# A two-layer graph network on one core: fewer semaphore signals per tile, and a node's own row as one product and one sum over types

## What is computed

```
h = max(layernorm(x), 0)
for l in range(3):                                   # W_rel (3, 8, 256, 256)
    xr  = einsum('nd,rde->rne', h, W_rel[l])
    msg = xr[edge_type, src]
    agg = segment_sum(msg, dst)
    h   = relu(agg + h @ W_root[l] + bias[l])
x = x + h
h = max(layernorm(x), 0) @ Wv + bv
e = (h @ wq + bq)[src] + (h @ wk + bk)[dst]
c = where(e > 0, e, 0.2 * e)
attn = softmax of c over the edges of one dst
x = x + segment_sum(h[src] * attn, dst)
```

## Time and profile before

| | us |
|---|---|
| median of 3 runs | 4443.56 (4443.05 to 4451.2) |
| span of the profiled execution | 5279.0 |
| first gather of pass 0, 1, 2 and attention starts at | 370.55, 1594.04, 2781.71, 3949.97 |
| last gather starts at | 5241.22 |
| busy: PE, ACT, DVE, POOL | 3562.7, 2197.4, 1645.5, 3082.0 |

### The profile page before, as it was taken

How to read it: one execution, slowest core, us unless ns; L and a number is a source line. 1 busy time by engine, 2 the same in 40 slices (tenths; PEclk the granted TensorE clock), 3 DMA queues, 4 the chain that set the end, 5 groups by cost and what they waited for, 6 DMA issues and landing times.

```text
span 5279.0 us, 56334 instructions
## 1 busy us (share of the span) xinstructions
PE 3562.7 (67%) x12674; PEld 2487.8 (47%) x12674; DVE 1645.5 (31%) x4423; ACT 2197.4 (42%) x6033; POOL 3082.0 (58%) x3322
## 2 busy tenths in 40 slices
PE   9986878787784777777784545555545566666656
PEld 4444555455552545444553334433434455555445
DVE  4533333333431212212121111111113444454444
ACT  2332334344333444334433333333334555565555
POOL 1145666666646666666646666666645555566554
PEclk9997888888896888888896777777776777887778
DMA  6554555555544444444433333333323333333332
GB/s 210 196 195 131 190 173 191 176 187 183 188 156 126 138 132 138 132 138 130 140 125 104 102 102 106 103 103 104 103 81 87 88 91 86 95 103 97 87 88 76
DMA packets 241011, 684.11 MB, mean 130 GB/s; under 512 B 60504, under 2 KB 112308, under 8 KB 215988
## 3 DMA queue, kind: packets, MB, share of 16 engines
q0 software_dynamic: 153360, 421.67, 27.9%
q10 hardware_dynamic: 57240, 186.43, 9.5%
q1 hardware_dynamic: 30092, 72.34, 3.8%
HBM read 504.62 MB, written 175.58 MB: 129 GB/s over the span
## 4 chain that ended last, share of the span: by engine, by line
PE 36%; another core or an unknown queue 29%; ACT 14%; issue 13%; DVE 6%; ACTq 1%; DVEq 0%; DMA 0%; SPq 0%
PE bank L1544 15%; PE sum_ps L1630 11%; ACT masks L1449 5%; PE sum_ps L1744 4%; ACT masks L1355 4%; PE bank L1700 2%; DVE root L806 2%; PE bank L1694 2%; ACT wide L1426 2%; ACT masks L1363 1%; PE turn_ps L1529 1%; PE sum_ps L1623 1%; ACT stage L1465 1%; ACT stage L1262 1%
## 5 line engine op out<-in xcount | busy, mean ns | idle before, releaser
L590 POOL DMA_INDIRECT ring<-table,code x2376 | 2258.3, 950 | 1324.9 <-issue 725.7
L1630 PE MATMUL sum_ps<-ring,masks 128*128 x5292 | 1404.4, 423 | 220.3 <-issue 208.5
L1630 PEld LDWEIGHTS sum_ps<-ring,masks 128*128 128x128 f32 x5292 | 1124.9, 215 | 473.6 <-issue 292.5
L1544 PE MATMUL bank<-wide,xT 128*128 128x512 f32 (+1 forms) x2744 | 1124.1, 564 | 1.4 <-ACT xT L1253 1.4
L590 POOL DMA_INDIRECT ring<-h_table,code x792 | 751.4, 949 | 576.7 <-SPq L730 326.5
L1355 ACT ACTIVATE masks<-node_row,local 128x128 f32<-128x128 f32 x2646 | 788.0, 388 | 24.8 <-issue 10.8
L1544 PEld LDWEIGHTS bank<-wide,xT 128*128 128x128 f32 x2744 | 515.1, 190 | 556.3 <-issue 544.9
L1744 PE MATMUL sum_ps<-ring,stage 128*128 x1764 | 525.5, 448 | 323.4 <-ACT stage L1465 163.1
L1253 ACT ACTIVATE xT<-turn_ps 128x256 f32<-128x256 f32 x196 | 75.6, 386 | 1461.2 <-remote 710.5
L1744 PEld LDWEIGHTS sum_ps<-ring,stage 128*128 128x128 f32 x1764 | 381.4, 229 | 391.2 <-issue 337.6
L1262 ACT COPY stage<-bank 128x512 f32<-128x512 f32 x441 | 242.5, 585 | 647.1 <-remote 436.2
(11 more groups left out here) (218 smaller groups left out, 2497.4 us busy)
## 6 DMA issues: line engine op xcount, KB each, us to landing
table<-stage ACTq DMA_DIRECT2D x96, 1024.0 KB
back<-table ACTq DMA_DIRECT2D x49, 1024.0 KB
table<-stage SPq DMA_DIRECT2D x48, 1024.0 KB
ring<-table,code POOLq DMA_INDIRECT x2376
ring<-h_table,code POOLq DMA_INDIRECT x792
h_table<-stage ACTq DMA_DIRECT2D x49, 130.0 KB
back<-h_table ACTq DMA_DIRECT2D x49, 130.0 KB
features<-xT SPq DMA_DIRECT2D x49, 128.0 KB, 4.0
```

The lines of the kernel that those rows point to most:

```text
L590: pool.indirect_dma_start(slot(c % RING, width), None, table, bass.IndirectOffsetOnAxis(ap=code[:, c:c + 1], axis=0)).then_inc(landed[n % ...
L1544: last = nc.tensor.matmul(bank[q][:, 0:width], xT[:, b, k, :], weights[:, k, 512 * q:512 * q + width], start=(k == 0), stop=(k == K - 1))
L1630: last = nc.tensor.matmul(sum_ps[b][:, 0:D], masks[:, b, s, :], at_offset(slots[s]), start=(s == 0 and l > 0), stop=(s == SLOTS - 1))
```

## The change

It does five things.

1. PE signals `added` twice a tile, after the pieces 1 and 4, not five times. The count of parts that a ring group needs (`need`), which SP waits for before it signals `released`, is built from two steps: one part if the tile has begun, two if the group's last chunk lies 8 or more past the tile's first.
2. In the transforms of passes 0 and 1 PE signals after the second bank and at the end, and waits for the previous tile's banks once at the start (`banks_copied`, `banks_read`). ACT signals its three copies once, DVE its copy once. The bias is added by a further matmul into the fifth bank, one row of ones times one row of bias, 256 columns.
3. ACT signals a mask twice instead of ten times.
4. The own row, for the table of the next pass: DVE waits until all four banks are in `stage`, multiplies the 2048 columns of `stage` by `loops` (each weight repeated over 256 columns) into `back`, reduces over the types into `root`, and adds the fifth bank. For the rows loaded back in pass 0 the same: one product in place in `back`, one sum, one addition. `back` has one load buffer now, and ACT's loads move behind the table's store.
5. Small ones: the last tile of a pass is stored in two DMAs, not four; two dot products in the projection follow each other with one wait; seven steps of POOL's preparation go.

The diff, cut to what the prediction speaks of:

```
+    PART_ENDS = (1, PIECES - 1)
+    PARTS = len(PART_ENDS)
+    SECOND_PART = (PART_ENDS[0] + 1) * GROUP
...
+        loaded_back = back[:, 0, :].rearrange("p (r d) -> p r d", r=R)
+        weighted = back[:, 1, :].rearrange("p (r d) -> p r d", r=R)
...
+            step(pool.tensor_tensor(need_sum, need_sum, tiles_to.unsqueeze(1).to_broadcast(full_n), ALU.mult))
+            step(pool.tensor_scalar(past, past, float(SECOND_PART), None, ALU.is_ge))
+            pool.tensor_tensor(need_sum, need_sum, past, ALU.add).then_inc(plan_marked, 1)
...
+            def evacuate(l, i, use, b):
+
+                tiles = (l - 1) * NT + i
+                q = R // 2 - 1
+                dve.wait_ge(transformed[b], transforms(use, b) + 2)
                 dve.wait_ge(stored[b], table_stored(l, b, use))
...
+                nc.vector.tensor_copy(stage[:, b, 512 * q:512 * (q + 1)], bank[q][:, :]).then_inc(banks_read, 1)
+                dve.wait_ge(banks_read, CREDIT + tiles + 1)
+                dve.wait_ge(banks_copied, CREDIT + tiles + 1)
+                in_order_step(nc.vector.tensor_tensor(weighted, by_type(stage[:, b, :]), loop_weights(i), ALU.mult))
+                in_order_step(nc.vector.tensor_reduce(root[:, i, :], over_types(weighted), AX.X, ALU.add))
+                nc.vector.tensor_tensor(root[:, i, :], bank[NB - 1][:, 0:D], root[:, i, :], ALU.add).then_inc(rooted, 1)
...
-                for t in range(R):
-                    if t:
-                        settle(dve, loops_done(i, t))
-                        dve.wait_ge(back_step, loops_done(i, t))
-                    nc.vector.scalar_tensor_tensor(root[:, i, :] if t == R - 1 else loop_ps, back[:, b, t * D:(t + 1) * D],
-                                                   loop_weight(i, t), loop_ps if t else root[:, i, :], ALU.mult, ALU.add
-                                                   ).then_inc(back_step, 1)
...
+                nc.vector.tensor_tensor(loaded_back, loaded_back, loop_weights(i), ALU.mult).then_inc(back_step, 1)
+                dve.wait_ge(back_step, 3 * i + 1)
+                nc.vector.tensor_reduce(loop_sum[:, :], over_types(loaded_back), AX.X, ALU.add).then_inc(back_step, 1)
+                dve.wait_ge(back_step, 3 * i + 2)
+                nc.vector.tensor_tensor(root[:, i, :], loop_sum[:, :], root[:, i, :], ALU.add).then_inc(back_step, 1)
+                dve.wait_ge(back_step, 3 * i + 3)
...
+            def evacuate(l, i, use, b):
+                tiles = (l - 1) * NT + i
+                if tiles > 1:
+                    act.wait_ge(rooted, CREDIT + tiles - 1)
+                act.wait_ge(stored[b], table_stored(l, b, use))
+                for q in range(R // 2 - 1):
+                    act.wait_ge(transformed[b], transforms(use, b) + (1 if q < EARLY else 2))
+                    last = nc.scalar.copy(stage[:, b, 512 * q:512 * (q + 1)], bank[q][:, :])
+                last.then_inc(banks_copied, 1)
...
+            def load_back(l, i, b):
+                if l:
+                    return
+                if i:
+                    act.wait_ge(back_step, 3 * i - 1)
+                act.dma_start(back[:, 0, :], tables_by_node[0][bass.ds(i * P, P), :]).then_inc(back_loaded[b], 16)
...
+                pe.wait_ge(rooted, CREDIT + tiles)
+                for k in range(K):
+                    nc.tensor.matmul(bank[NB - 1][:, 0:D], xT[:, b, k, :], weights[:, k, R * D:(R + 1) * D],
+                                     start=(k == 0), stop=False)
+                nc.tensor.matmul(bank[NB - 1][:, 0:D], ones[0:1, :], bias_row[0:1, :], start=False, stop=True
+                                 ).then_inc(transformed[b], 1)
...
-                    last.then_inc(added, 1)
+                    if c in PART_ENDS:
+                        last.then_inc(added, 1)
```

More of the change, by code:

```diff
@@ L724, in relay @@
                             _, counts = nc.values_load_multi_w_load_instructions(
-                                need[0:1, m:end], engines=[sp.engine], min_val=1, max_val=NT * PIECES,
-                                skip_runtime_bounds_check_because="counts of pieces, largest over the tiles")
-                        value = (counts[m % BATCH] & AT_MOST_PIECES) + (CREDIT + l * NT * PIECES)
+                                need[0:1, m:end], engines=[sp.engine], min_val=1, max_val=NT * PARTS,
+                                skip_runtime_bounds_check_because="counts of parts, largest over the tiles")
+                        value = (counts[m % BATCH] & AT_MOST_PARTS) + (CREDIT + l * NT * PARTS)
                         settle(sp, value)
@@ L733, in _ @@
                 for q in range(NB):
-                    sp.wait_ge(evacuated[q], CREDIT + NT * (l + 1))
+                    sp.wait_ge(evacuated[q], CREDIT + NT)
+                for tiles_done in (banks_copied, banks_read, rooted):
+                    sp.wait_ge(tiles_done, CREDIT + NT * l)
                 for b in range(2):
@@ new lines, in evacuate_first, with by_type, over_types, loop_weights @@
+                nc.vector.tensor_copy(stage[:, b, 512 * q:512 * (q + 1)], bank[q][:, :]).then_inc(evacuated[q], 1)
+                nc.vector.tensor_copy(root[:, i, :], bias_row[:, :]).then_inc(evacuated[NB - 1], 1)
+            def by_type(of):
+                return of.rearrange("p (t d) -> p t d", d=D)
+            def over_types(of):
+                return of.rearrange("p t d -> p d t")
+            def loop_weights(i):
+                return loops[:, i, :].unsqueeze(2).to_broadcast([P, R, D])
@@ L1530, in turn, with transform_first @@
                 last.then_inc(turned[b], 1)
-            def transform(step, use, b, banks, first=False, lead=False, between=None):
-                found = None
+            def transform_first(step, use, b, banks):
                 if banks[0] == 0:
@@ L1539, in transform @@
                         pe.wait_ge(first_weights[q], 16 * K)
-                    if not first and q < R // 2 and not lead:
-                        pe.wait_ge(root_step, loops_done(step - NT - 1, 2 * q + 2))
-                    width = min(512, (R + 1) * D - 512 * q)
                     for k in range(K):
-                        last = nc.tensor.matmul(bank[q][:, 0:width], xT[:, b, k, :],
-                                                weights[:, k, 512 * q:512 * q + width],
+                        last = nc.tensor.matmul(bank[q][:, :], xT[:, b, k, :], weights[:, k, 512 * q:512 * (q + 1)],
@@ L1546, in transform @@
                                                 start=(k == 0), stop=(k == K - 1))
-                    last.then_inc(transformed[b], 2 if first and q == NB - 2 else 1)
+                    last.then_inc(transformed[b], 2 if q == NB - 2 else 1)
+            def transform(tiles, use, b, between=None):
+                found = None
+                pe.wait_ge(xT_ready[b], use + 1)
+                pe.wait_ge(banks_copied, CREDIT + tiles)
+                pe.wait_ge(banks_read, CREDIT + tiles)
+                for q in range(NB - 1):
+                    for k in range(K):
+                        last = nc.tensor.matmul(bank[q][:, :], xT[:, b, k, :], weights[:, k, 512 * q:512 * (q + 1)],
+                                                start=(k == 0), stop=(k == K - 1))
+                    if q == EARLY - 1:
+                        last.then_inc(transformed[b], 1)
@@ L1647, in _ @@
                 pe.wait_ge(weights_loaded, weights_of(l + 1))
+                for q in range(NB):
+                    pe.wait_ge(evacuated[q], CREDIT + NT)
                 sum_tile(l, load_plan(pe, 0), 0, 0)
```

223 lines of the change are left out of this document (86 added, 137 removed).

## The result

The changed kernel takes **4701.4 us** (4696.0 to 4702.5, four runs) against 4445.9 for the kernel before in the same comparison: a ratio of 1.057, with a 95% interval of 1.055 to 1.058. It is slower by some 255 us, and 41 us above the forecast, inside its range. A second comparison gave 4697.8 against 4444.7, a ratio of 1.057 again.

The account below looks back on a forecast made before the run. POOL's gather stream was taken as the bound, PE close behind. 4443.6 + 208 (gathers held by products) + 5 (PE's period) + 3 (pass boundaries) = 4660 us, 4.9% slower; range 4555 to 4770.

Parts of the forecast that it names:

- What bounds the kernel: POOL's gather stream bounds the measured time: 3168 gathers of 1.25 us, 3960 us of the median 4443.6.
- the 753 us of late signals: POOL's extra waiting for SP's releases in the trace, from PE's late signals, belongs mostly to the traced execution.
- forecast of the traced span: Profiled span of the changed kernel: 5279 to 5490 us, since POOL's waiting can take the holds up.
- The product: DVE's own-row multiplication over 2048 columns in passes 0 and 1 takes 2.29 us, extrapolated from 256 and 832 columns.
- The hold: Each two-SBUF-input product holds one POOL gather until it ends: 143 times 1.46 us, 208 us.
- The reduction: DVE's sum over the types behind each product takes about 2.3 us, with 2.1 to 4 us as ends.
- PE's period: PE's tile grows from 17.45 to 19.8 us at full clock, 21 to 22 as granted; adds 5 us, 0 to 30.
- PE decides, no hold: Rival: gathers are hardly held, PE's 21 to 22 us a tile adds 80 to 170 us, 4520 to 4600; chance 0.07.
- The boundaries: Between passes, the last tile's table is stored some 1.5 us later, twice: +3 us.
- Coarser releases, added waits, fewer signals: SP's later releases, new waits of ACT and PE, and fewer signals of PE, ACT and DVE: zero each.
- cap on the hold: Rival: a product holds a gather at most 0.25 us, 36 us in all; chance 0.07 if PE decides, otherwise 0.03 plus 0.02.
- The late signals: Rival: PE's signals lag unprofiled too, so fewer signals gain 280 us: 4160, or up to 4430; chance 0.07.

Follow-up runs that it names:

- before_again: The kernel before, unchanged, run and traced again on a chip where it is at its faster level: 4453.0 us, span 4450.4.
- z_first: Changed kernel with the own row's reduction and addition issued behind z of the next tile: 5260.1 us, 1.001; on a faster chip 4685 us, 1.053.
- after_again: The changed kernel as it is, run again: 4697.8 us against 4444.7 for the kernel before.
- by_column: Changed kernel with the product written column by column, so the reduction reads contiguous columns and the product writes with a stride: 5460.5 us, 1.038.
- one_input_b: Changed kernel with each product replaced by an equally long one-input reduction, own row's weights left out, on a faster chip: 4668 us, 1.049.
- chain: Changed kernel with the own row made again by eight dependent instructions, one SBUF input beside PSUM; loaded rows likewise, from a single buffer: 4587.4 us, 1.032.
- fine_releases: chain_z_first with PE's signals for each piece of a sum again, five a tile: 4495.7 us, 1.009.
- chain_z_first: chain with its eight instructions behind z of the next tile, loaded rows in two buffers, their partial sum in the fifth bank: 4495 us, 1.010.
- one_input_z_first: Changed kernel with products replaced by one-input reductions, weights left out, and the strided reduction behind z of the next tile: 5213.3 us, 0.993.

## Why the prediction came out right, and where its steps did not

**What bounds the kernel: right, by a wrong step.** POOL's stream of 1.25 us gathers bounds the 4444 us, and `before_again` shows it directly: 991.8 to 997.2 us a pass. The prediction put the 753 us of late signals down to "mostly the traced execution". Profiling doesn't make them: on a quiet chip they are missing from the trace too, and on the other the kernel before takes 800 us more without a profiler. That the result was measured on a quiet chip was luck as far as this step goes: on the late-signal chip the sum wouldn't have applied, and the variant `z_first` is level there. For the same reason the forecast of the traced span, 5279 to 5490, was wrong: it is 4699.0.

**The product: right.** 2.29 us predicted, 2.292 measured, 147 times. The step from 256 and 832 columns to 2048 was sound.

**The hold: right, in law, number and size.** Predicted were 143 holds of 1.46 us, 208 us; there were 142 of 1.53 us, 218 us, and in `after_again` 143 of 1.50 us, 214 us. In `after_again` 145 gathers began during a product. Two began within 0.03 us of its start and weren't held, as the prediction had it for the first 0.08 us; the other 143 each lasted to the product's end plus 0.82 us, to within 0.01 us. So what the earlier trace rows showed up to 0.48 us goes on to 2.29, as the prediction took from the Trainium skill (SBUF — State Buffer, "SBUF: two separate sides"). The other half of that rule, that whichever starts first shuts the other out, doesn't show here: 114 of the 147 products of `after_again` began while a gather was running, took 2.28 to 2.32 us like the rest, and left that gather at 0.95. No reduction held one, strided or not.

**The reduction: mis-sized.** 2.3 us taken from the nearer row, 3.62 and 3.72 measured. "Its strided order isn't in the trace", with 4 us as the upper end, was where the choice went wrong; `by_column` shows that the order makes the difference, 2.29 against 3.6 to 3.9 us. The Trainium skill has the rule, and the prediction didn't weigh it: SBUF is read and written in lines of 16 bytes, four float32, and each access that crosses to a new line pays (SBUF — State Buffer, "Door 1: The DMA port swizzle"). A stride of 256 or 8 float32 crosses each time, and both came out slow.

**PE's period: too short, and priced too low.** The prediction made `z` 1.5 to 2 us later, PE's period 19.8 us at full clock and 21 to 22 at the clock of rows 8, and added 5 us. PE's wait grew from 0.57 to 3.05 us, 2.5 later, mostly because the reduction takes 1.3 us more; the bias takes two records and 0.69 us. At full clock the period is 20.7 us, and with the clock that was granted 22.2 to 22.4. That is 2.0 to 2.2 us over POOL's 20.2, in 98 tiles some 210 us, and it accounts for the 217 that `one_input_b` loses. The rival "PE decides, no hold" had 80 to 170 us for this. The boundaries, where PE catches up, grew by 34 us in the first trace of the changed kernel (28.8 and 49.4) and 26 in the second, where 3 and PE's 5 were foreseen. The 41 us between forecast and result are then, by the first trace: 26 us of boundaries above those 8, 9 of short waits of POOL, and 6 that the holds and the point where the sum began leave over (it began at 4443.6, the kernel before took 4445 to 4455 in the later comparisons).

**The way of adding up: the total right, the attribution half.** The sum is a maximum of two chains in each tile. The prediction treated it so, but took PE for the shorter one by a margin it didn't have: the holds came first, PE as a small rest. In pass 0 it had it right. In pass 1 its total came out by luck: PE alone gives 1110.6 us there and the holds alone 1088.4, only 22 us apart. A reader of the sum would have concluded that the kernel is repaired once the holds are gone. It isn't: 4668.

**Coarser releases, added waits, fewer signals: nothing, as said, where it was tried.** `chain` shows it for pass 1, `fine_releases` for the releases. For pass 0 it isn't shown: the cause of the 44 us of `chain_z_first` is open, and moving ACT's loads behind the store, which the prediction priced at zero, is the first suspect.

**The rivals.** No cap on the hold. The late signals are real, but on chips where the kernel before takes 5250 us; whether the change would gain there wasn't measured, and of its variants `z_first` is level and `one_input_z_first` 0.7% faster.

## What to carry to other kernels

Beside a stream of gathers an instruction of DVE with two SBUF inputs should be short, or be cut: four of 512 columns cost 37 us where one of 2048 cost 226. When a reduction has to walk with a stride, look for it before joining small instructions into one, and put the result that others wait for (`z` here) ahead of the work that can wait. And where two engines' chains are nearly equal, an experiment must take both causes away, together and singly; one alone shows next to nothing of either. A wait that leaves PE idle has to be priced with the clock that was granted, not at full clock: 20.7 us a tile became 22.2 to 22.4.

## What the runs showed that I had not expected

The condition of a chip can matter more than the change. The same kernel before takes 4445 to 4455 us in four comparisons and 5247 in one; the granted clock of its runs was 0.884 to 0.890 beside `chain_z_first` and 0.810 to 0.823 in that one. On the late-signal chip ACT follows PE's transposes of pass 2 some 11 us late while POOL issues gathers, as in the earlier trace rows; in passes 0 and 1 it follows them at once there too (0.04 us after their end in the median). In the quiet traces it never lags by more than 1.7 us. Here in `before_again`, in pass 2:

```profile
3225.98 0.38 PE L1529 MATMUL turn_ps<-ident,z 128*128 128x128 f32 x2
...
3226.39 0.39 ACT L1253 ACTIVATE xT<-turn_ps 128x256 f32<-128x256 f32 x1 [10.06 <-PE turn_ps L1529]
```

0.41 us from start to start. What makes a chip one or the other these runs don't tell, nor whether the lower clock there is a cause or a result. But an experiment's price depends on it (a late `z` without holds: 194 us on the one, 173 on the other; the holds beside an early `z`: 47 and 190), so kernels are to be compared on one chip, in one comparison.
